# A feature-interaction tower on one core: the first chunk's rows gathered by quarters of the batch, and its wide items set ahead of the first tiles' units

## What is computed

```python
e = stack([tbl_f[ids[:, f]] for f in range(40)], axis=1)        # 2048 x 40 x 64
z = einsum('bie,fie,bif->bi', e[:, row], param, e[:, col])      # 780 pairs
h = concatenate([z, dense_ctx], axis=1)
h = maximum(h @ W_top1 + b_top1, 0)                             # 796 -> 512
h = maximum(h @ W_top2 + b_top2, 0)                             # 512 -> 256
y = h @ W_top3
```

## Time and profile before

| | us |
|---|---|
| median of 3 runs | 1275.88 (1272.23 to 1280.07) |
| the profiled execution | 1274.63 |
| its span, first to last instruction | 1272.8 |
| PE busy | 1231.0 (97%) |
| DVE busy | 1023.4 (80%) |
| ACT busy | 1023.9 (80%) |
| POOL busy | 577.7 (45%) |

### The profile page before, as it was taken

How to read it: one execution, slowest core, us unless ns; L and a number is a source line. 1 busy time by engine, 2 the same in 40 slices (tenths; PEclk the granted TensorE clock), 3 DMA queues, 4 the chain that set the end, 5 groups by cost and what they waited for, 6 DMA issues and landing times.

```text
span 1272.8 us, 23705 instructions
## 1 busy us (share of the span) xinstructions
PE 1231.0 (97%) x6064; PEld 481.1 (38%) x6064; DVE 1023.4 (80%) x1680; ACT 1023.9 (80%) x7945; POOL 577.7 (45%) x615
## 2 busy tenths in 40 slices
PE   6788999999999999999999999999999999999999
PEld 3233433333333343333344333433343333343333
DVE  5768999998887777888787887788889787788980
ACT  0049988777488989998958999899968898999981
POOL 5555555555555555555345555555225554000000
PEclk9989999999999999999999999999999999999999
DMA  6311422132221222222221222122112122111100
GB/s 173 94 46 46 143 72 70 45 94 64 71 70 48 70 71 70 49 67 64 66 67 47 73 69 71 45 70 72 54 59 69 46 70 67 30 47 50 44 2 0
DMA packets 33201, 80.88 MB, mean 64 GB/s; under 512 B 11773, under 2 KB 12285, under 8 KB 32937
## 3 DMA queue, kind: packets, MB, share of 16 engines
q1 hardware_dynamic: 12320, 57.17, 13.9%
q0 software_dynamic: 19456, 19.96, 7.7%
q10 hardware_dynamic: 1288, 2.24, 0.6%
HBM read 79.32 MB, written 0.01 MB: 62 GB/s over the span
## 4 chain that ended last, share of the span: by engine, by line
PE 60%; ACT 31%; issue 3%; DMA 2%; POOL 2%; DVE 1%; another core or an unknown queue 1%; ACTq 0%
ACT wide_prod L541 29%; PE ring L727 26%; PE z_ps L750 13%; PE ring L732 11%; PE ring L756 7%; DMA rows<-tbl,idx_now 2%; POOL rows L481 2%; PE ring L701 2%; ACT e_t L502 1%; PE ring L760 1%; DMA idx_now<-idx 0%; DVE prod L606 0%; PE ring L763 0%; PE ring L708 0%
## 5 line engine op out<-in xcount | busy, mean ns | idle before, releaser
L541 ACT ACTIVATE wide_prod<-wide_prod 128x64 f32<-128x64 f32 x3904 | 933.7, 243 | 52.4 <-DVE wide_prod L619 25.6
L481 POOL DMA_INDIRECT rows<-tbl,idx_now x608 | 576.9, 949 | 496.7 <-DMA rows<-tbl,idx_now 292.2
L541 ACT ACTIVATION_READ_ACCUMULATOR wide_prod<-wide_prod 128x1 f32 x3904 | 739.4, 189 | 24.4 <-issue 23.4
L606 DVE TENSOR_TENSOR prod<-ring,e_t 128x512 f32<-128x512 f32 x1008 | 630.8, 683 | 147.6 <-PE ring L727 101.1
L727 PE MATMUL ring<-e_t,w 64*128 64x512 f32 x2176 | 563.0, 609 | 9.6 <-ACT e_t L502 5.9
L619 DVE TENSOR_TENSOR wide_prod<-ring,rows 128x512 f32<-128x512 f32 x512 | 328.3, 682 | 44.6 <-PE ring L732 33.3
L727 PEld LDWEIGHTS ring<-e_t,w 64*128 64x128 f32 x2176 | 215.9, 187 | 300.1 <-issue 203.7
L732 PE MATMUL ring<-w,e_t 64*128 64x512 f32 x1024 | 292.1, 607 | 11.4 <-ACT e_t L502 7.1
L750 PE MATMUL z_ps<-prod,strip 128*32 128x512 f32 x2096 | 256.2, 603 | 0.1
L732 PEld LDWEIGHTS ring<-w,e_t 64*128 64x128 f32 x1024 | 106.2, 186 | 147.0 <-issue 86.7
L750 PEld LDWEIGHTS z_ps<-prod,strip 128*32 128x32 f32 x2096 | 55.3, 109 | 182.0 <-issue 119.6
(11 more groups left out here) (23 smaller groups left out, 79.3 us busy)
## 6 DMA issues: line engine op xcount, KB each, us to landing
w<-weights SPq DMA_DIRECT2D x64, 768.0 KB
rows<-tbl,idx_now POOLq DMA_INDIRECT x608
w<-weights SPq DMA_DIRECT2D x4, 512.0 KB
z_t<-tbl SPq DMA_DIRECT2D x8, 224.0 KB
w<-w1z SPq DMA_DIRECT2D x1, 1792.0 KB
h<-hot_ids ACTq DMA_DIRECT2D x6, 256.0 KB
z_t<-hot_ids ACTq DMA_DIRECT2D x2, 256.0 KB
w<-w2p SPq DMA_DIRECT2D x1, 512.0 KB
```

The costliest lines, as they stand in the source:

```text
L481: nc.gpsimd.indirect_dma_start(out=rows[:, slot, t, E * f:E * f + E], out_offset=None, in_=tables[m * 2 + f], in_offset=bass.IndirectOffse ...
L541: last = nc.scalar.activation(products, products, ACT.Copy, accum_out=z_b[:, h, t, col:col + 1])
L606: nc.vector.tensor_tensor(dst[:, j, :], ring[:, bank, :], e_t[:, k, :], ALU.mult).then_inc(t_free, 1)
```

## The change

In the first chunk only:

- the gathers of tiles 0 to 3 go quarter by quarter: all 8 tables for quarter 0, then all for quarter 1, and so on, with a semaphore `rows_in[t]` for each quarter. It is the same 32 gathers, with a wait after the first 8 and then after each 4, as before;
- the wide items of tiles 4 to 7 need only the rows of their quarter. They move between and behind the units of rows 5 to 7, ahead of the units of rows 1 to 3; those units move to items 22 to 31. From item 32 on the list is as it was;
- tiles 0 and 1 are turned at item 20, tiles 2 and 3 at item 24 (before: 8, 10 and 12), and tiles 8 to 19 some items later than before (`LEAD`), tile 8 at item 30 and tile 9 at 36;
- the one-hot masks lie in four slots of `prod` in place of `wide_prod`; the masks of tile 6 are written ahead of item 2 and those of tile 7 ahead of item 4 (before: tile 6 ahead of item 0, tile 7 ahead of item 2);
- SP loads piece 1 right behind the tables, and pieces 2 and the second index table when quarter 2 has landed; piece 3 waits for item 21 (before: item 11).

```diff
-HOT_AT = {0: (4, 5, 6), 2: (7,)}
+HOT_AT = {0: (4, 5), 2: (6,), 4: (7,)}
+HOT_SLOTS = 4
+LEAD = [2, 4, 6, 7, 8, 10, 12, 12, 14, 14, 14, 14]
...
-    hot = [item for item in units if UNITS[item[1]][0] in ONE_HOT]
-    items = hot + units[:head]
-    for m in range(FIXED, TILES):
-        row = [item for item in units if UNITS[item[1]][0] == m and item not in hot]
+    items = row(5) + [wide(4, 0), wide(5, 0)] + row(6) + [wide(6, 0)] + row(7) + [wide(7, 0)]
+    items += [wide(m, t) for t in (1, 2) for m in ONE_HOT]
+    items += [wide(4, 3), wide(5, 3)] + row(1) + [wide(6, 3)] + row(2) + [wide(7, 3)] + row(3)
+    for m in range(ONE_HOT[-1] + 1, TILES):
...
-        first = FIRST_OF[0, 5 if m == 4 else max(m, 1)]
-        return first if m <= ONE_HOT[-1] else first - m
+        if m < FIXED:
+            return PLACE[0, "wide", WIDES.index((ONE_HOT[0] + 2 * (m // 2), BT - 1))]
+
+        first = FIRST_OF[0, max(m, 5)]
+        return first if m <= ONE_HOT[-1] else first - LEAD[m - ONE_HOT[-1] - 1]
...
-        hot = [wide_prod[0:HOT_P, q // 2, q % 2, :] for q in range(2 * WIDE_SLOTS)]
+        hot = [prod[0:HOT_P, PROD_SLOTS - HOT_SLOTS + q // 2, q % 2, :] for q in range(2 * HOT_SLOTS)]
...
-            sp.wait_ge(transposed, T_NUMBER[0] + 1)
+            load(1)
+
+            sp.wait_ge(rows_in[2], 2 * FIXED * 16)
+            for piece in range(2, W_SLOTS):
+                load(piece)
             load_idx(1)
-            for piece in range(1, W_SLOTS):
-                load(piece)
...
+            for t in range(BT):
+                for m in range(FIXED):
+                    for f in range(2):
+                        gather(0, m, f, t, fixed_slot(0) + m, rows_in[t])
+                    if m % 2 == 1 and (t > 0 or m > 1):
+
+                        pool.wait_ge(rows_in[t], 16 * 2 * (m + 1))
+            for tile in GATHERED[FIXED:]:
...
+                if c == 0 and m in ONE_HOT:
+
+                    dve.wait_ge(rows_in[t], 2 * FIXED * 16)
...
-                pe.wait_ge(gathered[slot], use * 2 * BT * 16)
+                if tile >= FIXED:
+                    pe.wait_ge(gathered[slot], use * 2 * BT * 16)
                 dst = take_bank(("tile", tile))
                 for t in range(BT):
+                    if tile == 0:
+
+                        pe.wait_ge(rows_in[t], 2 * FIXED * 16)
```

42 lines of the change are left out of this document (25 added, 17 removed).

## The result

| | median of runs | lowest to highest | profiled run: time, span |
|---|---|---|---|
| before | 1274.95 us (22 runs) | 1270.61 to 1280.07 | 1274.6, 1272.8 us |
| after | 1279.36 us (22 runs) | 1271.98 to 1286.23 | 1286.23, 1284.4 us |

The ratio is 1.0034 (95% interval 1.0018 to 1.0050): 4.4 us slower, where I had forecast 1.9 us faster. The profiled execution of the changed kernel is the longest of its 22, 6.9 us above their median, so the trace shows the loss enlarged; its place is plain all the same.

The account below looks back on a forecast made before the run. TensorE bounds the steady part, with GpSimd's gathers tightest at item 220. A start gain of 11.8 us shrinks to 5.3 there, less 3.4 for the clock: 1.9 us, new median 1274.0 us, range 1267.5 to 1278.5.

Parts of the forecast that it names:

- The start: Chunk 0 up to item 32: VectorE begins that item at 97.6 instead of 109.39 us, gaining 11.8 us, bounds 8 to 16.
- The in-order queue of ScalarE: At item 20 and after: copies of tiles 2 and 3 stand behind quarter 2's four sums, until 86.4 us.
- The gathers: Landing of tile 29: load collisions sum to -1.5 us, bounds -5 to +5, so 358.0 in place of 359.5 us.
- piece 1: 768 KB load joining the first DMA burst: delays the gathers by 0 to 2.9 us, taken as +1.4.
- the three loads: Loads that hit the seventh group of gathers: they are gone from there, taken as -3.7 us, or -1.9 if half stays.
- Piece 3, +0.8: Weight load at about 71 us beside tile 8's gathers: costs them 0 to 1.8 us, taken as +0.8.
- The tower's weights: Their load meets the gathers at another phase: plus or minus 2 us, middle 0.
- The rule of the Trainium skill: DMA engines serve gather and load queues in turn: piece 1's term would be 0, the sum below 1.4 us better.
- The new wait and its clock: Item 220, tile 29: TensorE waits 6.5 us, leaving 5.3 us of gain; the clock's fall costs 3.4, net 1.9.
- The one without a fall of the clock: Rival at item 220: wait under 5 us, clock doesn't fall, gain about 5.3 us, 1270.6 us; chance 0.22.
- The gathers come later: Rival: tile 29 lands 4.7 us later, at 364.2; 4.3 us slower with the clock, 1280.2 us; chance 0.12.
- the old collision: Term of the later-gathers rival: 3.7 us at the gathers, replaced by one of like size from a load inside the next group.

## Why the prediction was wrong

- **The bound.** The reading held: what the start gains must pass the gathers at items 212 to 230. "At item 220 the rows are only 3.8 us ahead of TensorE" was the right place to look.
- **The start.** Forecast 11.8 us at item 32, with bounds of 8 to 16; measured 9.0 (100.44 against 97.6). The in-order queue of ScalarE came as worked out: the copies of tiles 2 and 3 start at 86.7, TensorE waits 3.1 us for tile 2's, VectorE 2.9 us behind it at 89.41, and the clock's mean from 80 to 110 us is 0.83. Nearly all of what is missing lies in this one step. I had VectorE at row 2 at 86.7, right behind the copies, and left out the matmuls that TensorE makes in between; it came there at 89.41, and from there to item 32 it takes 11.0 us, where I had 10.9. The slow clock, which I kept for the bounds, is a part of this step only: two units took 3.64 us at 87.30 against 1.96 at 91.64, so some 0.8 us for the first of them.
- **The gathers: the step that failed.** I summed collisions to -1.5 us, with bounds of 5 to either side, and tile 29 came 9.9 us later. By its own terms: piece 1 and the three loads, +1.4 and -3.7, gave -1.1 and not -2.3 by the first half of tile 8 (71.4 against 72.4). Piece 1 moved the first landing by 0.4 us, and the three loads' delay is gone; but two groups, from 28.6 and 36.6 us on, take 1.6 and 2.0 us more than 6.41, where they took 0.4 and 0.8 before. No load of SP is under way in them, so their cause is open. Piece 3, +0.8, measured 1.5. The tower's weights, "middle 0", 5.8 us against 4.2, are 1.6 more. With 0.8 us from a group near 100 us this makes 3.0 us by tile 14. The other 6.9 us came between 163 and 369 us from a term that I hadn't written at all and so had put at nothing: a dozen ordinary weight loads, which follow TensorE, and so by the change hit the gathers' groups at other phases. Before, groups with such a load took 1.3 to 1.8 us more four times; after, 0.9 to 2.9 us six times, and 1.0 us once without a load.
- **The rule of the Trainium skill** (DMA: Bandwidth & Descriptors, section SWDGE vs HWDGE vs iDMA), that each DMA engine serves both kinds of queue in turn. The waits agree in kind: a load under way lengthens a gather's wait, 7.50 us against 1.76, and doesn't block it until its end, for the tower's packets run to 132.9 us and the gathers had landed before 131.3 (in the kernel before the packets end at 140.5 and the gathers landed before 141.1, which tells neither way). That the gathers wouldn't need to wait for piece 1 is borne out too but for 0.4 us: the first wait ends at 21.91 against 21.54, and the load's last packet at 23.3.
- **The new wait and its clock.** I had one wait of 6.5 us and a fall of the clock of 3.4 us at tile 29. There is one of 6.2 us there, one of 5.0 us at tile 27 besides, and 4.0 us of clock for both. I hadn't looked at tile 27: in the trace before it landed at 333.6, ahead of its turn at 346.39 by 12.8 us, which a lead of 9.1 us and a lateness of 9.9 us more than use up.
- **The rivals.** The one without a fall of the clock took it that a wait under 5 us has none. The runs say otherwise: the clock was halved after waits of 4.39 and 2.75 us. "The gathers come later" had the mechanism and the sign, and 1280.2 us against 1279.4, but its terms, piece 1 and the old collision, weren't what came, so the time is in part luck; I gave it 0.12 since I took the sum's middle for what is likely, where each of its terms was the phase of a load that the trace before could not tell.
- What stays open: the size of the loss in the first session. The profiled runs differ by 11.6 us, 7.7 of them at tile 31 and 3.9 later, the medians by 4.4.

## What to carry to other kernels

A lead won at the start is worth only what the next independent stream lets through: find that stream (here GpSimd's gathers), its slack at each place where the fast engine meets it, and count every load that moves with the fast engine into its path, not only those the change touches. If a group of small transfers is waited for as a whole, start large loads right at its landing, or better, wait for the group one transfer behind, which here was worth more than the whole change. And before two orders are compared by half a per cent, look whether both wait at the same place, and in which of their executions: here one wait for rows was worth as much as the whole change.

## What the hardware showed that I had not expected

- **Phase.** By the traces of this case, what a load of 768 KB costs a group of four gathers (6.4 us) depends on when it starts: mostly 0 to 0.3 us if in the first 1.5 us or the last 0.6, mostly 0.9 to 2.9 us if 2.5 to 4.3 us into it.
- **Delays without a load.** Four groups of the changed kernel's trace, from 28.6, 36.6, 98.5 and 217.0 us on, take 1.0 to 2.0 us more than 6.41 with no load of SP beside them. Each has a packet of the trace's instruction queues within it (at 34.3, 37.7, 103.9 and 222.9 us, 8 or 16 KB). Whether that is the cause wasn't tested.
- **Eight gathers under way** made the two kernels 29 and 32% slower in the second session, with stops of VectorE and ScalarE of up to 15 and 17 us for a cause outside the trace; five or six in a later session cost nothing. Eight weren't run in a later session, nor six in one of the first two, so I can't say whether the number or the session decides. That it is the supply of instructions, which also comes by DMA, is argued, not shown.
- **Sessions.** The first session's trace of the kernel before has 36 gaps of over 0.6 us on ScalarE, VectorE and TensorE with no cause in it ("issue" or "remote"), such as this one in the timeline of ScalarE:

```profile
699.68 0.60 ACT L502 ACTIVATE e_t<-ring 128x512 f32<-128x512 f32 x1 [3.68 <-remote]
```

In the later session it has two (5.1 us at the very start and 0.7 us), and from tile 31 to the last tile it takes 773.5 us in place of 804.3. The gathers' pace is the same in both, 12.9 us a tile.
